# The store of a group's outputs, issued on ScalarE's queue instead of SyncE's

## The reference, cut to what matters

```python
q = (hidden_states @ Wq).reshape(B, Sq, 20, 16).transpose(0, 2, 1, 3)
k = (encoder_hidden_states @ Wk).reshape(B, 1024, 20, 16).transpose(0, 2, 1, 3)
v = (encoder_hidden_states @ Wv).reshape(B, 1024, 20, 16).transpose(0, 2, 1, 3)
probs = softmax(einsum('bhqd,bhkd->bhqk', q, k) / sqrt(16))
out = einsum('bhqk,bhkd->bhqd', probs, v)
out = out.transpose(0, 2, 1, 3).reshape(B, Sq, 320) @ Wo + bo + residual
```

## Time and profile before

| what | value |
|---|---|
| time, median of three runs | 325.64 us (325.45 to 331.66) |
| the profiled execution's own time | 327.17 us |
| its span, first to last instruction | 325.3 us |
| mean granted TensorE clock | 0.99 |
| PE busy | 310.9 us (96%) |
| DVE busy | 262.0 us (81%) |
| ACT busy | 229.2 us (70%), 468 instructions |
| POOL busy | 78.4 us (24%) |

### The profile page before, as it was taken

How to read it: one execution, slowest core, us unless ns; L and a number is a source line. 1 busy time by engine, 2 the same in 40 slices (tenths; PEclk the granted TensorE clock), 3 DMA queues, 4 the chain that set the end, 5 groups by cost and what they waited for, 6 DMA issues and landing times.

```text
span 325.3 us, 6083 instructions
## 1 busy us (share of the span) xinstructions
PE 310.9 (96%) x2086; PEld 167.7 (52%) x2086; DVE 262.0 (81%) x456; ACT 229.2 (70%) x468; POOL 78.4 (24%) x97
## 2 busy tenths in 40 slices
PE   7999997999999999999999999999999999999995
PEld 6678886876667634334343434433334453434324
DVE  1479899779996879989999999999899988893213
ACT  3556455443445778889879878898798876888982
POOL 6065166242434400010014100040441016101030
PEclk9999999899999979999999999999999999999999
DMA  7960008629956741191540915509146111110102
GB/s 219 312 208 0 3 1 210 217 92 157 224 184 209 166 100 55 43 139 33 127 90 34 148 36 114 102 33 151 34 104 104 40 40 38 50 38 28 37 29 82
DMA packets 20193, 32.79 MB, mean 101 GB/s; under 512 B 5539, under 2 KB 9667, under 8 KB 20163
## 3 DMA queue, kind: packets, MB, share of 16 engines
q1 hardware_dynamic: 19075, 31.27, 40.9%
q10 hardware_dynamic: 1088, 1.14, 1.2%
HBM read 20.63 MB, written 11.61 MB: 99 GB/s over the span
## 4 chain that ended last, share of the span: by engine, by line
PE 66%; DVE 11%; ACT 9%; issue 6%; DMA 5%; SPq 3%; POOL 0%; ACTq 0%; DVEq 0%; POOLq 0%
PE ps L1393 19%; PE ps L1370 13%; PE ps L1381 13%; PE ps L1221 10%; PE ps L1042 5%; ACT probs L701 4%; DVE mx L906 3%; ACT probs_last L701 3%; SPq L347 2%; DMA QS<-mT 1%; DMA rec_rows<-recs 1%; DMA xs<-in_x_dram 1%; PE ps L1148 1%; DVE max L845 1%; DMA QS<-q_parts 1%
## 5 line engine op out<-in xcount | busy, mean ns | idle before, releaser
L906 DVE TENSOR_REDUCE mx<-ps 128x1 f32<-128x512 f32 x298 | 186.0, 683 | 17.9 <-PE ps L1370 16.7
L701 ACT ACTIVATE probs<-ps 128x512 f32<-128x512 f32 x216 | 113.5, 609 | 22.3 <-PE ps L1381 20.8
L1370 PE MATMUL ps<-KS,QS 48*128 48x512 f32 x256 | 78.4, 453 | 2.1 <-ACT probs L701 1.2
L1381 PE MATMUL ps<-QS,KS 50*128 50x512 f32 x256 | 72.0, 442 | 1.9 <-DMA QS<-mT 0.9
L1393 PE MATMUL ps<-probs,VS 128*32 128x512 f32 (+1 forms) x552 | 61.0, 517 | 0.3 <-ACT probs L701 0.3
L701 ACT ACTIVATE probs_last<-ps 128x512 f32<-128x512 f32 x104 | 54.7, 608 | 8.3 <-PE ps L1381 7.7
L1370 PEld LDWEIGHTS ps<-KS,QS 48*128 48x128 f32 x256 | 35.3, 185 | 37.6 <-DVE mx L906 17.0
L1381 PEld LDWEIGHTS ps<-QS,KS 50*128 50x128 f32 x256 | 34.1, 187 | 33.4 <-ACT probs L701 13.3
L507 POOL CAST neg_p<-neg 128x16 fp32r<-128x16 f32 x10 | 2.1, 213 | 113.2 <-DVE neg L916 107.6
L1393 PE MATMUL ps<-probs_last,VS 128*32 128x512 f32 (+1 forms) x256 | 29.0, 524 | 0.0
L683 ACT CAST parts<-ps 128x512 fp32r<-128x512 f32 (+1 forms) x18 | 10.5, 585 | 23.6 <-PE ps L1221 23.4
(11 more groups left out here) (186 smaller groups left out, 444.9 us busy)
## 6 DMA issues: line engine op xcount, KB each, us to landing
KS<-k_parts SPq DMA_DIRECT2D x48, 128.0 KB, 4.6
k_parts<-parts SPq DMA_DIRECT2D x8, 512.0 KB, 3.6
QS<-q_parts SPq DMA_DIRECT2D x48, 64.0 KB, 4.7
raw_rows<-o_raw SPq DMA_DIRECT2D x9, 256.0 KB, 2.0
q_parts<-parts SPq DMA_DIRECT2D x4, 512.0 KB, 3.2
cs<-in_ctx_dram SPq DMA_DIRECT2D x2, 768.0 KB, 9.3
KS_last<-k_parts SPq DMA_DIRECT2D x12, 128.0 KB, 4.6
xs<-in_x_dram SPq DMA_DIRECT2D x2, 640.0 KB, 6.5
```

The source lines that it names most:

```text
L701: act.activation(probs[t % 3][:, h, :], ps[:, bank_of["s", m], :], ACT.Exp, scale=float(D1) ** -0.5).then_inc(exp_done, 1)
L906: dve.tensor_reduce(mx[:, g % BUF, u:u + 1], ps[:, bank_of["m", n], :], AX.X, ALU.max).then_inc(max_done, 1)
L1370: pe.matmul(ps[:, bank, :], QS[g % BUF][rows, pair, qt * P:(qt + 1) * P], KS[g % BUF][rows, pair, half * 512:half * 512 + 512], start=True ...
L1381: pe.matmul(ps[:, bank, :], KS[g % BUF][rows, h // 2, kt * P:(kt + 1) * P], QS[g % BUF][rows, h // 2, :], start=True, stop=True).then_inc( ...
```

## The change

For groups 0 to 7 the store of `o_raw` is taken from SP's program and put into ACT's, behind the copy. Since a DMA may only read what has been written, ACT first waits for its own copy's semaphore. SP keeps the store of group 8, whose copy is on DVE, and keeps its wait for `o_sent` ahead of the read of the denominators.

```diff
             def send_outputs(g):
 
-                sp.wait_ge(o_copied, g + 1)
-                sp.dma_start(raw_rows[g], o_raw[:, :]).then_inc(o_sent, 16)
+                if g == NG - 2:
+                    sp.wait_ge(o_copied, g + 1)
+                    sp.dma_start(raw_rows[g], o_raw[:, :]).then_inc(o_sent, 16)
                 if g >= 2:
                     sp.wait_ge(recs_done, g - 1)
                 sp.wait_ge(o_sent, 16 * (g + 1))
...
                 act.copy(o_raw[:, :], ps[:, bank_of["pv", g], :]).then_inc(o_copied, 1)
+                act.wait_ge(o_copied, g + 1)
+                act.dma_start(raw_rows[g], o_raw[:, :]).then_inc(o_sent, 16)
```

## The result

The changed kernel is slower, by less than two per cent: 1.0147 times the kernel before, 95% interval 1.0117 to 1.0177. In the first measurement its median was 334.12 us (330.77 to 341.58, four runs) beside 328.65 for the kernel before (325.45 to 333.46); the ratio compares executions near each kernel's fastest and leaves out those more than 1.5% above it, the medians hold all. The direction was right and the forecast ratio, 329.7 / 325.64 = 1.0125, lies in the interval, but 334.12 lies outside the range of 326.7 to 331.5.

The account below looks back on a forecast made before the run. The prediction took the kernel to be bound by PE's written order, with little room anywhere. Delays of 3.5 (six groups), 0.5 (group 6) and 0.07 (group 2) sum to 4.1; 325.64 + 4.1 = 329.7 us, range 326.7 to 331.5.

Parts of the forecast that it names:

- The detour: On ACT, groups 0 to 7: the next exponential starts 1.05 after the copy's start instead of 0.47, 0.58 us later.
- Passed to the end: Delays on the chain through ACT reach the end: 3.5 us from six groups, 0.5 from group 6, 0.07 from group 2.
- the six groups named: Groups 0, 1, 3, 4, 5 and 7, where the chain runs through ACT: each passes 0.58 us, 3.5 in all.
- The step that let 0.49 be taken up in group 2: In group 2, PE's 0.49 us idle for SP's late rows of maxima takes up the delay; 0.07 passes.
- Absorbed in part: Rival: ACT's later idle time catches up, share 0.37 passes, costing 1.7 us: 327.3; chance 0.22 for 326.4 to 329.
- Not slower: Rival: detours fall into PE's other work and SP's series in group 2 gains up to 0.34: 325.3 to 326.0; chance 0.08.
- Gain: 0: On SP: the issue of 0.34 per group was covered by its wait for the landing, so removing it gains nothing.
- The dear issue: Rival: each issue on ACT takes 0.74, detour 0.93, sum 6.9 us: 332.5; chance 0.08 for 330.3 to 333.
- the sum goes onto that median: Last step: adds 4.1 us to the median of the runs shown, 325.64, not to the profiled execution's 327.17, giving 329.7.
- the sum of 4.05: Predicted delays of all eight groups together, 4.05 us in the table, given as 4.1 in the prediction.

Follow-up runs that it names:

- pair at full clock: One trace each of the unchanged kernel before and the changed kernel, both at clock 1.000: spans 322.5 and 325.1 us.
- The second copy: Kernel before plus a second same-size copy on ACT behind the copy of groups 0 to 7, no wait or DMA added: ratio 1.0194.
- the late store: Changed kernel with ACT's wait and store moved behind the first of the four exponentials that follow the copy: ratio 0.9966.
- wait alone: Kernel before with ACT's wait for its own copy added and the store left on SP: ratio 1.0006.
- copy behind the second exponential: Kernel before, store on SP, with ACT's copy behind the second of the four exponentials in all groups but group 2: ratio 1.0179.
- with the change: The version listed just ahead, with wait and store also on ACT: ratio 1.021 for the moved copy; no ratio for SP's moved wait, median 335.92 us.
- SP's wait moved: Kernel before with SP's wait for the inverses' landing and the load behind it two steps later, groups 0 to 5: ratio 1.0141.
- two issues: Changed kernel with each of ACT's stores split into two halves of 64 rows: ratio 1.0572.

## Why the prediction was right in its mechanism and wrong in its time

**The detour.** Predicted 0.58, measured 0.56 to 0.62. Two terms were off against each other: the issue took 0.33 and not 0.39 (SP's price for this transfer was the right row), and 0.09 passed behind it and not 0.04. That the two cancel is luck.

**Passed to the end.** In the pair at full clock right in five of the six groups named, and in group 6 (0.44 for 0.5). The second copy, with neither wait nor DMA, shows that it is the delay of the exponentials that passes, and the late store that without the delay nothing is paid.

**Group 2 and group 4.** The step that let 0.49 be taken up in group 2 rested on one execution's wait for the rows of maxima. That wait wanders: it depends on the landing of the inverses, on which SP stands (4.4 us in the first trace, 3.1 in the one at full clock). Only the first of the four traces of the kernel before has it; their third distances are 20.33, 19.83, 19.81 and 19.92. Against that first trace group 2 came out near the forecast (20.22, 0.11 less, for 0.07 more), in the pair at full clock it passed 0.41. Group 4, which I had let pass in full, passed 0.09, because there the kernel before waited for the rows of maxima, in all four traces (0.43 to 0.74). The trace behind the prediction had this wait too, 0.43, and the prediction counted such a wait in group 2 alone:

```profile
233.55 0.49 PE L1381 MATMUL ps<-QS,KS 50*128 50x512 f32 x1 [0.43 <-DMA QS<-mT]
```

In the pair at full clock it was, before:

```profile
230.76 0.50 PE L1381 MATMUL ps<-QS,KS 50*128 50x512 f32 x1 [0.56 <-DMA QS<-mT]
```

and in none of the four traces of the changed kernel did PE wait there. PE and ACT's copy of the rows came later by the detour, but SP needs two issues for the rows, and they had moved together; SP's rows for this group, before and changed:

```profile
227.57 1.72 SPq L374 DMA_DIRECT2D QS<-mT  x2
```

```profile
228.99 1.39 SPq L374 DMA_DIRECT2D QS<-mT  x2
```

The second issue starts 1.05 or 1.06 behind the first in all seven traces in which SP's program is the one of the kernel before, and 0.73 or less in the eleven others. So the second half of the rows was issued only 0.2 later behind the copy. Why the two issues lie closer, no run shows. The errors in groups 2 and 4 nearly cancel, 3.86 against 4.05: that the sum of this pair comes so near is in part luck.

**The rivals.** Absorbed in part: not as a common share of 0.37; in the pair six groups passed 0.44 to 0.60, and group 4 lost its detour to SP's rows, not to ACT's later idle time. Not slower: SP's series behind the store had no 0.34 to win, since it waits for the landing as long as before; the 0.33 between the two issues in group 4 is a gain on SP that the prediction, with "Gain: 0", had not. The dear issue: didn't come, 0.33 at all eight.

**The step that failed** is the last one of the sum, "the sum goes onto that median", with the range drawn around it. It takes the clock of the one trace and the median of three runs for given; the granted clock has no term and no rival, although the page had one to read. The first trace's span of 325.3 itself holds two stretches at half clock, at 56 and 114 us (a granted 0.95 and 0.92 in the stretches around them); the one at 56 begins as PE resumes from 1.43 of idle time. The change lengthens PE's waits behind the copies, in groups 0 and 1 from 0.66 and 0.79 to 1.21 and 1.35, in groups 3 and 5 from 0.13 and 0.20 to 0.66 and 0.77, and gives the clock more places to fall. How often over all executions whose clock is listed, under a clock of 0.985: before 0 of 72, wait alone and late store 0 of 12 each, copy behind the second exponential 0 of 6, with the change 2 of 6, changed kernel 7 of 19, SP's wait moved 4 of 6, with the change 3 of 6, second copy 5 of 6, two issues 6 of 6. A short stretch (3.4 us) costs about 1.5 (2.05 - 0.57 in group 0), the long one of ten 4.0 and more (4.6 - 0.1 to 0.6 in group 4). The median of 334.12 is one with half its four executions in that condition (0.964 and 0.953, at 337.35 and 341.58); the two others, 330.77 and 330.9, lie inside the range. The base moved too, and by more: its median of four is 328.65, not 325.64, which is 3.0 of the 4.4 by which 334.12 lies above 329.7. The clocks of these four aren't listed, so what made two of them long stays open. Put onto 328.65 the sum gives 332.7, still outside the range.

**What stays open.** At full clock the medians of the spans lie 2.35 apart, not 3.86. Up to the first copy, ahead of any change, full-clock executions take 129.7 to 131.0, so a pair can differ by 1.3 there without the change: this one does, the other way (129.73 against 130.99). And the kernel before may at full clock wait longer for the rows of maxima than in the two traces (the versions with the wait alone and the late store, at 0.7 and 0.8, did so in the fourth distance). No trace here shows an execution of it with a span over 323 at full clock, so this isn't settled. The two edits meant to remove that wait (SP's order) brought a new one instead.

## What to carry to other kernels

A DMA issued right behind its producer on ScalarE cost that engine the wait, the issue and the lost overlap, 0.6 us here for an issue of 0.33; with one independent instruction of that engine between producer and store most of it was covered (0.15 was left). Read where the chain of waits enters and leaves the engine, then add the delay once for each place where it does, and look in every group for a wait that takes it up: the sum of 4.05 stands beside 3.86 in the pair at full clock and 2.35 between the medians. Before putting such a sum onto a median, look whether the granted clock in the trace is full, and whether the edit lengthens TensorE's waits; a forecast then needs a second case at the lower clock.

## What the runs showed of the hardware that was not expected

The clock of TensorE fell to half behind waits of 0.7 to 2.1 us inside work that is otherwise nearly gapless, in some executions and not in others, and stayed there for 3.4, 7, 10 and, in one trace each, 17 and 20 us. At 111 to 114 us it fell in two traces without such a wait. Useless products put into the wait made a kernel faster, from 1.0572 to 1.0316. And a store of 64 rows took longer to issue (0.45 and 0.61 us) than one of 128 rows (0.33) on the same queue. With eight issues taken out of SP's program two later issues of SP's stood, in one place, 0.33 us closer together.
